# The last attention step of a Flamingo block in an order of its own

## The chip, the cores and the metric

The kernel runs on one core of a Trainium2 chip. The metric is the time of one execution on the device in microseconds (us); before the change it is 874.02 us, the median of three runs (873.65 to 874.04).

A core has a TensorE (matrix products and transposes; its weight loads are a row of their own, PEld), a VectorE (DVE), a ScalarE (ACT), a GpSimd (POOL) and a SyncE (SP), which starts transfers. Each works off its own list of instructions in order and waits on semaphores for the others.

## The reference

`x` is 2 batches of 2048 rows of 512, the context 2 batches of 77 rows. A gated cross-attention of 16 heads of width 32 is followed by a gated feed-forward layer:

```python
x = x + tanh(g_xattn[0]) * xattn(layernorm(x), ctx, ctx, Wq, Wk, Wv, Wo)
x = x + tanh(g_ffn[0]) * ffn(layernorm(x), w_gate, w_up, w_down)
# xattn: softmax of (q k^T * HD**-0.5) over the 77 context rows, causal mask, times v, times Wo^T
# ffn:   silu(x wg^T) * (x wu^T), times wd^T; integer weights, scaled by 1/127
```

## The kernel before

Products of float32 values are made from a high part (rounded to fp32r) and a low part (the rest): ACT writes the high part of a result in PSUM to SBUF, DVE subtracts it from PSUM for the low part, and TensorE makes three products (high by high, low by high, high by low).

The 4096 rows go in NB = 8 blocks of 512, and a block in TT = 4 tiles of 128 rows. A block's **step** has four kinds of work on each tile t:

- **scores**: `score_unit(n, t, u)` makes six products of 308 columns for heads 0 to 7 (unit 0, PSUM banks 0 and 1) or 8 to 15 (unit 1, banks 2 and 3). Each unit has one pair of banks, so a tile's unit waits until the tile before it is out: unit 0 for the shift on DVE (`s0_shifted`), unit 1 for the exponentials on ACT (`exp1_done`).
- **softmax**. Unit 0: DVE takes the maxima (`mx`, L1073), subtracts them into `e` in SBUF (L1076, `shift0`), ACT makes one exponential of 616 columns (`exp0`, L784), DVE sums and inverts (`denominator0`). Unit 1: DVE takes the maxima (L1084, `largest1`) and makes their scaled negative (`nmx`, L1090, `offset1`), ACT makes eight exponentials of 77 columns straight from PSUM, with the sums (`exp1`, L791), DVE inverts them (L1114, `denominator1`). POOL multiplies `e` by the inverse, unit by unit (L554, `weigh`).
- **transposes** of the weighed `e` in three pieces, `p(t, 0)` and `p(t, 1)` of four 128-column transposes and `p(t, 2)` of two, through two PSUM banks in turn. ACT copies each piece to `pT` (L764), DVE makes its low part (L1047); only that frees the bank for the piece after the next. `p(t, 0)` waits for the weighing of unit 0, `p(t, 1)` for that of unit 1.
- **output slices** `o(t)` (`project`): twelve products of 512 columns of `aT`, the weighed values of the block before, with `Wo`, added to `x_res` by DVE (L1120, `residual`).

At the head of a step stand the products of the block before's probabilities with V (36 products, `values`); between the transposes of the other steps stand also the query products of the next block. The last step (n = 7) has no query products. In their place it has `turn`: 16 transposes of normalised rows `x2` for the feed-forward layer into PSUM banks 0 to 3, which wait for the last tile's exponentials; POOL normalises `x2` in this step (L679). After the last step come the values and output slices of block 7, then the feed-forward layer, whose products (L1814, L1864) fill the time to the end.

The order on each engine is written out by hand, in `step` of each engine's program. On DVE the order within a tile is: `shift` (both units), `p(t-1, 0)`, `denominator0`, `p(t-1, 1)`, an output slice, `denominator1`, `p(t-1, 2)`, and then the next tile. The functions and lines are these:

Of the kernel before, what the change touches and what calls it, by code (L numbers as in the profile page):

```python
# [5 lines left out]
def flamingo_gated_block(  # L6
# [34 lines left out]
    P = 128  # L41
# [65 lines left out]
    with ctx:  # L107
# [396 lines left out]
        def _(pool):  # L504
# [166 lines left out]
            def normalise_first(i):  # L671

                c = slice(TT * i, TT * i + TT)
                nc.gpsimd.tensor_scalar(nmean2[:, c], mv2[:, c, 0], -1.0, 0.0, ALU.mult, ALU.add).then_inc(nmean_ready, 1)
                pool.wait_ge(nmean_ready, i + 1)
                pool.wait_ge(rstd2_ready, i + 1)
                for t in range(TT):
# [7 lines left out]
            normalise_first(0)  # L685
            probabilities(NB - 1, 1)
            normalise_first(1)
            probabilities(NB - 1, 2)
            probabilities(NB - 1, 3)
# [40 lines left out]
        def _(act):  # L730
# [136 lines left out]
            def step(n, query):  # L867
                def p(t, r):
                    p_high(n, t, r, 3 * t + r)

                def weighted(m):
                    m_high(m_base(n) + m, m, aT[:, 0, m, :])

                exp0(n, 0)
                weighted(0)
                exp1(n, 0, lambda: weighted(1))
                weighted(2)
                weighted(3)
                if query:
                    for k in range(KD):  # L880
                        x_high_t(n + 1, k)
                q_at = m_base(n) + 8

                def q(m):
                    if query:
                        m_high(q_at + m, m, qT[:, 0, m, :])

                for t in (1, 2):
                    p(t - 1, 0)
                    exp0(n, t)  # L890
                    p(t - 1, 1)
                    exp1(n, t)
                    p(t - 1, 2)
                p(2, 0)
                exp0(n, 3)
                p(2, 1)
                exp1(n, 3, lambda: q(0))
                p(2, 2)
                if not query:
                    act.wait_ge(var_out, 16 * MH)  # L900
                    xv_copy(0, B11, b11_at)
                q(1)
                q(2)
                p(3, 0)
                q(3)
                p(3, 1)
                if not query:
                    b12_copy(0)
                p(3, 2)
# [23 lines left out]
            with act.Fori(1, NB - 1) as n:  # L933
                step(n, True)
            step(NB - 1, False)
# [93 lines left out]
        def _(dve):  # L1029
# [242 lines left out]
            def step(n, query, ahead):  # L1272
                def p(t, r):
                    p_low(n, t, r, 3 * t + r)

                def st(t):
# [7 lines left out]
                    elif query and not ahead:  # L1284
                        stats2(t // TT, t % TT)

                def q(m):
                    if query:
                        q_low(h_base(n) + 5 + m, m)
# [13 lines left out]
                p(0, 0)  # L1303
                denominator0(n, 1)
                p(0, 1)
                residual(n, 0)
                denominator1(n, 1)
                p(0, 2)
                st(0)
                if query:  # L1310
                    residual(n, 1)
                slot_free(n, 2)
                shift(n, 2)
                p(1, 0)
                denominator0(n, 2)
                p(1, 1)
                residual(n, 2 if query else 1)
                denominator1(n, 2)
                p(1, 2)
                st(1)  # L1320
                if query:
                    residual(n, 3)
                slot_free(n, 3)
                shift(n, 3)
                p(2, 0)
                denominator0(n, 3)
                p(2, 1)
                st(2)
                q(0)
                if not query:  # L1330
                    residual(n, 2)
                denominator1(n, 3)
                p(2, 2)
                if not query:
                    residual(n, 3)
                st(3)
                if not query:
                    xv_low(0, B11, b11_at)
# [4 lines left out]
                p(3, 0)  # L1343
# [3 lines left out]
                p(3, 1)  # L1347
                p(3, 2)
                if not query:
                    form(0, T1)  # L1350
# [608 lines left out]
```

## Time and profile before

| | |
|---|---|
| runs, median (lowest to highest) | 874.02 us (873.65 to 874.04) |
| the profiled execution, whole | 874.07 us |
| its span in the profile | 872.3 us |
| busy share of the span: PE, PEld, DVE, ACT, POOL | 98%, 81%, 75%, 53%, 46% |
| granted TensorE clock, mean | 1.00 (2.4 GHz) in every slice |
| the last step's first score product, first values product after the step, first feed-forward product | 313.11, 350.57 and 372.39 us |

The profile counts from the span's start. A row of the timeline gives the start, the time from the start of its first to the end of its last instruction, engine, line, operation, the tiles, the count, and in brackets how long the engine was idle before it and what released it. TensorE's ends are modelled, and the next product starts before the one before it has ended, so for TensorE the distance between two starts is the better measure.

### The profile page before, as it was taken

To read this page: it belongs to the slowest core of one execution; us is meant where nothing else is said; L and a number is where in the kernel's file an instruction comes from. 1 tells how busy PE (TensorE), PEld (TensorE's weight loads), DVE (VectorE), ACT (ScalarE), POOL (GpSimd) and SP (SyncE) were. 2 spreads that over 40 slices of the span, in tenths; PEclk is the share of its full clock that TensorE was granted. 3 is DMA by queue.
4 is the path that set the end of the run, shared out by engine and by line. 5 is a ranking of instruction groups with operands and counts; after the bars stand their busy time and mean duration, and the time that the engine had idled before them with its cause. 6 is when DMAs were issued, how large, how long until landed. Compare 5 with 4: busy or idle time off the path is not lost.

```text
span 872.3 us, 12869 instructions
## 1 busy us (share of the span) xinstructions
PE 855.0 (98%) x4087; PEld 707.9 (81%) x4087; DVE 652.8 (75%) x1081; ACT 460.5 (53%) x1130; POOL 402.3 (46%) x344
## 2 busy tenths in 40 slices
PE   8999999999999999999999999999999999999997
PEld 7678888888888887788888888888888888888876
DVE  5988877778786877679688478788487877587882
ACT  5687575666666757446056264165362364460550
POOL 4665555556564664437144444155253255251350
PEclk9999999999999999999999999999999999999999
DMA  9233847272728131567333256043265143243302
GB/s 334 73 109 118 276 152 248 84 240 93 233 97 277 68 113 51 198 235 265 115 123 133 96 190 249 12 165 121 79 248 182 47 164 113 96 166 116 97 31 98
DMA packets 60406, 128.73 MB, mean 148 GB/s; under 512 B 7616, under 2 KB 20416, under 8 KB 60352
## 3 DMA queue, kind: packets, MB, share of 16 engines
q1 hardware_dynamic: 58960, 125.95, 41.7%
q10 hardware_dynamic: 1392, 2.10, 0.7%
q8 instruction: 29, 0.48, 0.2%
q14 instruction: 25, 0.20, 0.1%
HBM read 99.93 MB, written 27.79 MB: 146 GB/s over the span
## 4 chain that ended last, share of the span: by engine, by line
PE 87%; DVE 6%; ACT 3%; issue 1%; DMA 1%; POOL 1%; ACTq 0%; DVEq 0%
PE psum L1814 34%; PE psum L1548 29%; PE psum L1864 18%; PE psum L1573 4%; DMA gates<-g_ffn 1%; PE psum L1657 1%; ACT e L791 1%; POOL hT L696 1%; DVE bn L1034 1%; DVE e L1076 1%; DVE K L1128 1%; DVE mx L1073 1%; DVE qT L1058 0%; DVE pT L1047 0%; DVE aT L1058 0%
## 5 line engine op out<-in xcount | busy, mean ns | idle before, releaser
L1814 PE MATMUL psum<-xv,ring 128*128 128x512 f32 x1344 | 308.2, 390 | 0.9 <-ACT a L964 0.7
L1814 PEld LDWEIGHTS psum<-xv,ring 128*128 128x128 f32 x1344 | 251.5, 188 | 55.1 <-ACT a L964 1.1
L696 POOL TENSOR_TENSOR hT<-th,hT 128x512 fp32r<-128x512 f32 x48 | 86.3, 1798 | 201.2 <-ACT hT L984 201.2
L1864 PE MATMUL psum<-w_d,hT 128*128 128x512 f32 x768 | 177.7, 391 | 1.3 <-POOL hT L696 0.8
L1864 PEld LDWEIGHTS psum<-w_d,hT 128*128 128x128 f32 x768 | 143.7, 188 | 32.6 <-POOL hT L696 2.0
L554 POOL TENSOR_TENSOR e<-e,rden 128x616 f32<-128x616 f32 x64 | 77.9, 1217 | 110.4 <-DVE rden L1110 73.8
L791 ACT ACTIVATE e<-psum,nmx,q_scale 128x77 f32<-128x77 f32 x256 | 102.6, 427 | 2.3 <-DVE nmx L1090 2.2
L952 ACT ACTIVATE a<-psum 128x512 f32<-128x512 f32 x48 | 28.7, 599 | 131.7 <-PE psum L1814 131.4
L1428 DVE SCALAR_TENSOR_TENSOR acc<-psum,gate_ffn,acc 128x512 f32<-128x512 f32 x64 | 47.7, 750 | 65.1 <-PE psum L1864 65.1
L1548 PE MATMUL psum<-wo,aT 128*128 128x512 f32 x384 | 95.2, 399 | 0.5 <-DVE aT L1058 0.5
L1548 PE MATMUL psum<-xT,wq 128*128 128x512 f32 x360 | 89.0, 398 | 0.4 <-DVE qT L1058 0.4
L1548 PEld LDWEIGHTS psum<-wo,aT 128*128 128x128 f32 x384 | 70.0, 188 | 14.6 <-DVE aT L1058 0.8
L1548 PEld LDWEIGHTS psum<-xT,wq 128*128 128x128 f32 x360 | 65.6, 188 | 14.6 <-DVE qT L1058 1.9
L696 POOL TENSOR_TENSOR hT<-c,hT 128x512 fp32r<-128x512 f32 x48 | 62.1, 1293 | 22.4 <-ACT hT L984 22.4
L764 ACT ACTIVATE pT<-psum 128x512 fp32r<-128x512 f32 (+1 forms) x96 | 49.8, 531 | 36.2 <-PE psum L1573 36.2
L1548 PE MATMUL psum<-pT,V 128*128 128x512 f32 x288 | 68.1, 392 | 0.6 <-DVE aT L1058 0.6
L1548 PE MATMUL psum<-K,qT 128*128 128x308 f32 x384 | 63.7, 310 | 2.1 <-ACT e L791 2.1
L1548 PEld LDWEIGHTS psum<-pT,V 128*128 128x128 f32 x288 | 53.3, 188 | 12.5 <-DVE aT L1058 1.1
L1548 PEld LDWEIGHTS psum<-K,qT 128*128 128x128 f32 x384 | 56.8, 189 | 6.5 <-ACT e L791 3.0
L1392 DVE SCALAR_TENSOR_TENSOR th<-th,c 128x512 f32<-128x512 f32 x48 | 56.0, 1166 | 7.1 <-ACT th L977 4.3
L984 ACT ACTIVATE hT<-th 128x512 fp32r<-128x512 f32 x48 | 30.4, 633 | 53.9 <-DVE th L1405 53.9
L1047 DVE TENSOR_TENSOR pT<-psum,pT 128x512 fp32r<-128x512 f32 (+1 forms) x96 | 55.6, 588 | 2.5 <-ACT pT L764 1.0
(110 smaller groups left out, 1204.6 us busy)
## 6 DMA issues: line engine op xcount, KB each, us to landing
ring<-w_var SPq DMA_DIRECT2D x48, 896.0 KB, 4.6
w_var<-stage SPq DMA_DIRECT2D x12, 896.0 KB, 4.6
x_ln<-x SPq DMA_DIRECT2D x32, 256.0 KB, 4.6
x_res<-x SPq DMA_DIRECT2D x32, 256.0 KB, 5.0
x_mid<-x_res SPq DMA_DIRECT2D x32, 256.0 KB, 2.0
x<-x_mid SPq DMA_DIRECT2D x16, 512.0 KB, 5.6
acc<-x_mid SPq DMA_DIRECT2D x16, 512.0 KB, 6.4
out<-acc SPq DMA_DIRECT2D x32, 256.0 KB, 2.0
```

The source lines that it names most:

```text
L554: nc.gpsimd.tensor_tensor(e[:, t % 2, hs], e[:, t % 2, hs], rden[:, t % 2, hs].unsqueeze(2).to_broadcast([P, UH, SK]), ALU.mult).then_inc( ...
L696: nc.gpsimd.tensor_tensor(hT[:, 1, i % HH, j, :], h[:, :], hT[:, 0, i % HH, j, :].bitcast(f32), ALU.subtract).then_inc(h_lo, 1)
L764: nc.scalar.activation(dst, src, ACT.Copy).then_inc(t_hi, 1)
L791: last = nc.scalar.activation(e[:, t % 2, UH + h, :], s_bank[1][:, h // HG, (h % HG) * SK:(h % HG + 1) * SK], ACT.Exp, bias=nmx[:, t % 2, ...
L984: nc.scalar.activation(hT[:, 0, i % HH, j, :], h[:, :], ACT.Copy).then_inc(h_hi, 1)
L1047: nc.vector.tensor_tensor(dst, src, hi.bitcast(f32), ALU.subtract).then_inc(t_free, 1)
L1392: nc.vector.scalar_tensor_tensor(th2[:, :], th2[:, :], 1.0, c22[:, :], ALU.add, ALU.mult)\
L1428: nc.vector.scalar_tensor_tensor(acc[:, t, :], m_bank[t % 2][:, :], gate_ffn[:, 0:1], acc[:, t, :], ALU.mult, ALU.add).then_inc(m_free, 1)
L1548: last = nc.tensor.matmul(dst, stat, mov, start=(j == 0), stop=(j == len(terms) - 1))
L1573: last = nc.tensor.transpose(t_bank[at % 2][:, j * P:(j + 1) * P], rows[:, start:start + P], ident[:, :])
L1814: last = nc.tensor.matmul(psum[:, bank, :], stat, mov, start=start and j == 0, stop=j == len(terms) - 1, skip_group_check=not start)
L1864: last = nc.tensor.matmul(m_bank[t % 2][:, :], hT[:, a, m, t // TT, (t % TT) * P:(t % TT + 1) * P], w_d[:, HH * h + m, :], start=m == 0 an ...
```

## The change

Only the last step changes. It gets functions of its own on ACT, DVE and TensorE (`last_step`), and POOL's work there is put in another order; the loops of the other steps issue what they did. In the last step:

- TensorE: a tile's scores are no longer twelve products in a row. Unit 1 of tile t+1 stands behind `p(t, 0)`, unit 0 of tile t+2 behind `p(t, 2)`. An output slice goes in two halves of six products, one before `p(t, 1)` and one behind the scores of unit 0. `p(3, 0)` and the whole of `o(3)` stand ahead of `turn`.
- DVE: `p(t, 0)` stands between the shift of unit 0 and the maxima of unit 1; `p(t, 1)` and `p(t, 2)` stand together behind `denominator0`; `denominator1(t)` stands behind the shift of tile t+1, and the output slices one tile later.
- ACT: `p(t-1, 1)` is copied in the middle of the eight exponentials of tile t instead of ahead of them; `p(3, 0)` ahead of the copy of the turned rows.
- POOL: the negated means are made first; the second four normalisations of `x2` go in two pairs between weighings.

```diff
+                for t in (1, 2, 3):                       # ACT, last_step
+                    p(n, t - 1, 0)
+                    exp0(n, t)
+                    exp1(n, t, lambda: p(n, t - 1, 1))
+                    p(n, t - 1, 2)
...
+                for t in range(TT - 1):                   # DVE, last_step
+                    slot_free(n, t + 1)
+                    shift0(n, t + 1)
+                    if t:
+                        denominator1(n, t)
+                    p(n, t, 0)
+                    largest1(n, t + 1)
+                    offset1(n, t + 1)
+                    denominator0(n, t + 1)
+                    if t:
+                        residual(n, t - 1)
+                    p(n, t, 1)
+                    p(n, t, 2)
+                residual(n, 2)
+                p(n, 3, 0)
+                denominator1(n, 3)
+                residual(n, 3)
+                xv_low(0, B11, b11_at)
+                p(n, 3, 1)
+                p(n, 3, 2)
+                form(0, T1)
...
+                weigh_values(n, b, b, False)              # TensorE, last_step
+                score_unit(n, 1, 0, b, False)
+                for t in range(TT - 1):
+                    p(n, t, 0)
+                    score_unit(n, t + 1, 1, b, False)
+                    if t == 0:
+                        pe.wait_ge(m_free, base + 4)
+                    o(t, early)
+                    p(n, t, 1)
+                    p(n, t, 2)
+                    if t + 2 < TT:
+                        score_unit(n, t + 2, 0, b, False)
+                    o(t, late)
+                p(n, 3, 0)
+                o(3, range(G))
+                turn(0, B11)
+                turn(0, B12)
+                p(n, 3, 1)
+                p(n, 3, 2)
...
+            mean_first(0)                                 # POOL
+            mean_first(1)
             probabilities(NB - 1, 0)
+            normalise_first(0, range(TT))
+            weigh(NB - 1, 1, 0)
+            normalise_first(1, range(0, 2))
+            weigh(NB - 1, 1, 1)
+            weigh(NB - 1, 2, 0)
+            normalise_first(1, range(2, 4))
+            weigh(NB - 1, 2, 1)
+            weigh(NB - 1, 3, 0)
+            weigh(NB - 1, 3, 1)
```

The order on DVE before, from the last low part of tile 0 (`pT` of 2x128) to the offset of tile 2's unit 1 and what follows it. `mx` are maxima, `e` the shifted scores, `nmx` the offset, `rden` an inverse sum:

```order
L1114 RECIPROCAL rden<-den 128x8 [waits exp1_done]
L1047 TENSOR_TENSOR pT<-psum,pT 128x2x128 [waits t_hi]
L1073 TENSOR_REDUCE mx<-psum 128x8 [waits s0_full,t_full]
L1076 TENSOR_TENSOR e<-psum,mx 128x308 [waits mx0_done]
L1076 TENSOR_TENSOR e<-psum,mx 128x308
L1084 TENSOR_REDUCE mx<-psum 128x8 [waits s1_full]
L1090 SCALAR_TENSOR_TENSOR nmx<-mx,q_scale,minus 128x8 [waits mx1_done,scale_ready]
L1047 TENSOR_TENSOR pT<-psum,pT 128x4x128 [waits t_hi]
```

The same place on DVE now:

```order
L1067 TENSOR_TENSOR pT<-psum,pT 128x2x128 [waits t_hi]
L1093 TENSOR_REDUCE mx<-psum 128x8 [waits s0_full,t_full]
L1096 TENSOR_TENSOR e<-psum,mx 128x308 [waits mx0_done]
L1096 TENSOR_TENSOR e<-psum,mx 128x308
L1134 RECIPROCAL rden<-den 128x8 [waits exp1_done]
L1067 TENSOR_TENSOR pT<-psum,pT 128x4x128 [waits t_hi]
L1104 TENSOR_REDUCE mx<-psum 128x8 [waits s1_full]
L1110 SCALAR_TENSOR_TENSOR nmx<-mx,q_scale,minus 128x8 [waits mx1_done,scale_ready]
```

The inverse of tile 1's unit 1 moved from ahead of the shift of tile 2 to behind it, and it and the low part of `p(1, 0)` now stand ahead of the maxima and the offset of tile 2's unit 1. The low part of `p(0, 2)` still stands ahead of the shift.

The order on ACT before, from the shifted exponential of tile 2 to the last copy of tile 1 (`e,den` are the eight exponentials):

```order
L784 ACTIVATE e<-e,q_scale 128x616 [waits s0_shifted,scale_ready]
L764 ACTIVATE pT<-psum 128x4x128 [waits t_full]
L791 ACTIVATE e,den<-psum,nmx,q_scale 128x77 [waits nmx_ready]
L791 ACTIVATE e,den<-psum,nmx,q_scale 128x77 x7
L764 ACTIVATE pT<-psum 128x2x128 [waits t_full]
```

The same place on ACT now:

```order
L793 ACTIVATE e<-e,q_scale 128x616 [waits s0_shifted,scale_ready]
L800 ACTIVATE e,den<-psum,nmx,q_scale 128x77 [waits nmx_ready]
L800 ACTIVATE e,den<-psum,nmx,q_scale 128x77 x3
L773 ACTIVATE pT<-psum 128x4x128 [waits t_full]
L800 ACTIVATE e,den<-psum,nmx,q_scale 128x77 x4
L773 ACTIVATE pT<-psum 128x2x128 [waits t_full]
```

The copy of `p(1, 1)` moved from ahead of the eight exponentials to their middle; the copy of `p(1, 2)` stays behind the eighth.

The order on TensorE before, from tile 1's transposes to the last scores (`K,qT` are scores, `ident,e` transposes, `wo,aT` an output slice):

```order
L1573 MATMUL psum<-ident,e 128x128 [waits t_free,p0_ready]
L1573 MATMUL psum<-ident,e 128x128 x3
L1573 MATMUL psum<-ident,e 128x128 [waits t_free,p1_ready]
L1573 MATMUL psum<-ident,e 128x128 x3
L1548 MATMUL psum<-wo,aT 128x512 [waits m_free]
L1548 MATMUL psum<-wo,aT 128x512 x11
L1573 MATMUL psum<-ident,e 128x128 [waits t_free]
L1573 MATMUL psum<-ident,e 128x128
L1548 MATMUL psum<-K,qT 128x308 [waits s0_shifted]
L1548 MATMUL psum<-K,qT 128x308 x5
L1548 MATMUL psum<-K,qT 128x308 [waits exp1_done]
L1548 MATMUL psum<-K,qT 128x308 x5
```

The same place on TensorE now:

```order
L1613 MATMUL psum<-ident,e 128x128 [waits t_free,p0_ready]
L1613 MATMUL psum<-ident,e 128x128 x3
L1588 MATMUL psum<-K,qT 128x308 [waits exp1_done]
L1588 MATMUL psum<-K,qT 128x308 x5
L1657 MATMUL psum<-wo,aT 128x512 [waits m_free]
L1657 MATMUL psum<-wo,aT 128x512 x5
L1613 MATMUL psum<-ident,e 128x128 [waits t_free,p1_ready]
L1613 MATMUL psum<-ident,e 128x128 x3
L1613 MATMUL psum<-ident,e 128x128 [waits t_free]
L1613 MATMUL psum<-ident,e 128x128
L1588 MATMUL psum<-K,qT 128x308 [waits s0_shifted]
L1588 MATMUL psum<-K,qT 128x308 x5
```

The scores of unit 1, which wait for the exponentials of the tile before, moved from behind the output slice to behind `p(t, 0)`, and have half a slice behind them.

## Rows read from the trace of the kernel before

**Rows 1.** The page, busy time, share of the span and instructions of each engine

```profile
PE 855.0 (98%) x4087; PEld 707.9 (81%) x4087; DVE 652.8 (75%) x1081; ACT 460.5 (53%) x1130; POOL 402.3 (46%) x344
```

**Rows 2.** Timeline of TensorE over the last step: start, length, [idle before]

```profile
331.62 1.11 PE L1548 MATMUL psum<-K,qT 128*128 128x308 f32 x6 [1.19 <-ACT e L791]
...
338.51 1.13 PE L1548 MATMUL psum<-K,qT 128*128 128x308 f32 x6 [0.86 <-ACT e L791]
...
343.45 3.02 PE L1548 MATMUL psum<-wo,aT 128*128 128x512 f32 x12
...
350.38 0.44 PE L1573 MATMUL psum<-ident,e 128*128 128x128 f32 x2 [1.29 <-DVE pT L1047]
350.57 4.37 PE L1548 MATMUL psum<-pT,V 128*128 128x512 f32 x18
```

**Rows 3.** Chain that ended last, last step, in order of time: start, length

```profile
331.87 0.04 DVE pT L1047
...
332.21 0.80 DVE mx L1073
...
333.03 0.87 DVE e L1076 x2
...
335.29 3.18 ACT e L791 x16
```

**Rows 4.** Timeline of ACT: first exponentials of three tiles, copies around the second

```profile
328.28 0.41 ACT L791 ACTIVATE e<-psum,nmx,q_scale 128x77 f32<-128x77 f32 x1
...
334.71 0.58 ACT L764 ACTIVATE pT<-psum 128x512 fp32r<-128x512 f32 x1
335.18 0.41 ACT L791 ACTIVATE e<-psum,nmx,q_scale 128x77 f32<-128x77 f32 x1
...
338.33 0.40 ACT L764 ACTIVATE pT<-psum 128x256 fp32r<-128x256 f32 x1
...
342.08 0.41 ACT L791 ACTIVATE e<-psum,nmx,q_scale 128x77 f32<-128x77 f32 x1
```

**Rows 5.** Timeline of DVE: offsets of tiles 1 and 2, then tile 3

```profile
327.80 0.23 DVE L1090 SCALAR_TENSOR_TENSOR nmx<-mx,q_scale,minus 128x8 f32<-128x8 f32 x1
...
334.71 0.23 DVE L1090 SCALAR_TENSOR_TENSOR nmx<-mx,q_scale,minus 128x8 f32<-128x8 f32 x1
...
338.76 0.42 DVE L1047 TENSOR_TENSOR pT<-psum,pT 128x256 fp32r<-128x256 f32 x1
339.11 0.79 DVE L1073 TENSOR_REDUCE mx<-psum 128x8 f32<-128x616 f32 x1
...
340.71 0.79 DVE L1084 TENSOR_REDUCE mx<-psum 128x8 f32<-128x616 f32 x1
341.61 0.23 DVE L1090 SCALAR_TENSOR_TENSOR nmx<-mx,q_scale,minus 128x8 f32<-128x8 f32 x1
341.75 0.68 DVE L1047 TENSOR_TENSOR pT<-psum,pT 128x512 fp32r<-128x512 f32 x1
342.35 0.78 DVE L1108 TENSOR_REDUCE den<-e 128x8 f32<-128x616 f32 x1
343.17 0.20 DVE L1110 RECIPROCAL rden<-den 128x8 f32<-128x8 f32 x1
343.29 0.64 DVE L1047 TENSOR_TENSOR pT<-psum,pT 128x512 fp32r<-128x512 f32 x1
```

**Rows 6.** Timeline of POOL: four normalisations and a weighing in the last step

```profile
333.36 3.02 POOL L679 TENSOR_SCALAR x<-x,nmean,rstd 128x512 f32<-128x512 f32 x4
...
338.77 1.22 POOL L554 TENSOR_TENSOR e<-e,rden 128x616 f32<-128x616 f32 x1 [1.00 <-DVE rden L1114]
```

**Rows 7.** Timeline of SP's queue: reload of the rows for block 7's output slices

```profile
349.12 2.13 SPq L393 DMA_DIRECT2D x_res<-x  x4
```

**Rows 8.** Transfers issued from 345 to 362 us: KB each, us to landing

```profile
x_res<-x SPq DMA_DIRECT2D x4, 256.0 KB, 8.4
```

**Rows 9.** Timeline of DVE: first output slice of block 7

```profile
364.42 0.75 DVE L1120 SCALAR_TENSOR_TENSOR x_res<-psum,gate_t,x_res 128x512 f32<-128x512 f32 x1 [1.27 <-PE psum L1548]
```

More of the change, by code:

```diff
@@ L865, in first_block, with p @@
                 p(3, 2)
[L867 to L872, printed above, removed]
-                exp0(n, 0)
[L875 to L881, printed above, removed]
+            def p(n, t, r):
+                p_high(n, t, r, 3 * t + r)
@@ L1270, in xv_low, with p, step @@
                     .then_inc(xb_lo, 1)
[L1272 to L1274 removed]
+            def p(n, t, r):
+                p_low(n, t, r, 3 * t + r)
+            def step(n, ahead):
                 def st(t):
@@ L1610, in values, with project @@
                         ).then_inc(m_full, 1)
-            def project(i, t):
-                m_wait(i)
-                product(m_bank[t % 2][:, :],
-                        [(aT[:, a, m, t * P:(t + 1) * P], wo[:, c, m, :]) for m in range(G) for a, c in CROSS]
-                        ).then_inc(m_full, 1)
+            def project(i, t, groups=range(G)):
+                if groups[0] == 0:
+                    m_wait(i)
+                for m in groups:
+                    for a, c in CROSS:
+                        last = nc.tensor.matmul(m_bank[t % 2][:, :], aT[:, a, m, t * P:(t + 1) * P], wo[:, c, m, :],
+                                                start=m == 0 and a + c == 0, stop=m == G - 1 and c == 1)
+                if groups[-1] == G - 1:
+                    last.then_inc(m_full, 1)
             pe.wait_ge(const_step, 2)
@@ L1736, in first_block, with p, weigh_values, step @@
                 p(3, 2)
-            def step(n, b, b_before, masked, more):
+            def p(n, t, r):
+                transpose_p(n, t, r, 3 * t + r)
+            def weigh_values(n, b, b_before, masked):
+                scores(n, 0, b, masked, (m_base(n) - 2, m_base(n)))
+                for m in range(G):
+                    values(m_base(n) + m, m, b_before, t_base(n) - 2 + min(m, 2))
+            def step(n, b, b_before, masked):
                 base = m_base(n)
-                def p(t, r):
-                    transpose_p(n, t, r, 3 * t + r)
                 def o(t):
@@ L1747, in q @@
                 def q(m):
-                    if more:
-                        query(base + 8 + m, m)
-                scores(n, 0, b, masked, (base - 2, base))
-                for m in range(G):
-                    values(base + m, m, b_before, t_base(n) - 2 + min(m, 2))
+                    query(base + 8 + m, m)
+                weigh_values(n, b, b_before, masked)
                 scores(n, 1, b, False)
-                p(0, 0)
-                p(0, 1)
+                p(n, 0, 0)
+                p(n, 0, 1)
                 pe.wait_ge(m_free, base + 4)
```

171 lines of the change are left out of this document (88 added, 83 removed).

## The prediction

> **What bounds the kernel now.** I read the page's busy shares first: TensorE 98%, no other engine over 75% [rows 1]. A change gains only where TensorE stands, and it can lose wherever it makes TensorE stand longer. Then the timeline of TensorE over the last step, for its idle times: 1.19 us and 0.86 us before the scores of tiles 2 and 3, unit 1, both ended by ACT's exponentials of the tile before, and 1.29 us before the two last transposes, ended by a low part on DVE; the values products of block 7 begin at 350.57 [rows 2]. So 3.34 us are there to be had, 0.38% of the time. Then the chain of waits, to see what sets these stands: the low part of the two-piece product, the maxima and the shift of unit 0, and the eight exponentials follow one another, across DVE and ACT, round and round [rows 3]. ACT's timeline gives the loop's length: the first exponentials of tiles 1, 2 and 3 start at 328.28, 335.18 and 342.08, 6.90 us apart each time [rows 4]. This loop is the bound of the step, not TensorE.
>
> **The loop after the change, step by step.** ACT copies `p(t-1, 2)` only behind the eighth exponential of tile t, as before; DVE works in order, and its low part of that piece still stands ahead of the next shift. So "the shift sooner" holds for the scores that feed it, not for the shift. From one tile's first exponential to the next one's:
> - the eight exponentials, 338.33 - 335.18 = 3.15 [rows 4];
> - the copy of `p(t-1, 1)`, new in their middle: 335.18 - 334.71 = 0.47 [rows 4];
> - the copy of the two-piece part until DVE takes it: 338.76 - 338.33 = 0.43 [rows 4, 5];
> - its low part, 339.11 - 338.76 = 0.35 [rows 5];
> - maxima and shift of unit 0, 340.71 - 339.11 = 1.60 [rows 5];
> - the inverse of unit 1, now behind the shift: 343.29 - 343.17 = 0.12 (a reciprocal of the same size) [rows 5];
> - the low part of `p(t, 0)`, now ahead of the offset: 342.35 - 341.75 = 0.60 [rows 5];
> - maxima of unit 1 until the offset, 341.61 - 340.71 = 0.90 [rows 5];
> - the offset and the hand-over to ACT, 0.23 + 0.03 = 0.26 [rows 5].
>
> The sum is 7.88 us against 6.90. Before, the exponential of unit 0 and a copy on ACT ran beside the maxima and the offset; now they still do, and have ended a microsecond before the offset, so they hide nothing and cost nothing. What grew the loop are three things put on it: a copy between exponentials, a low part and an inverse before the offset.
>
> **Where the loop starts and where it meets TensorE.** In tile 1 the offset started at 327.80 and now stands behind the low part of `p(0, 0)`: 327.80 + 0.60 + 0.23 + 0.03 = 328.66 for the first exponential, 0.38 later than before. Tile 3's then starts at 328.66 + 2 x 7.88 = 344.42 (before 342.08). Behind its fourth exponential ACT copies `p(2, 1)`: 3.15 / 2 + 0.58 + 0.03 = 2.19 later [rows 4]; DVE's low part of it takes 0.68 [rows 5] and 0.05 of hand-over, and only that frees the bank for `p(3, 0)`, at 344.42 + 2.92 = 347.34. This is the new wait on TensorE. Queued behind it there are `o(3)`, the sixteen turns and six transposes, and then the values. The same instructions stood between 343.45 and 350.57 before, 7.12 us with 1.29 idle, so 5.83 of work [rows 2]. The values now start at 347.34 + 5.83 = 353.17, which is 2.60 later.
>
> TensorE is free by then. Tile 2's first exponential is at 336.54; the scores of tile 3 start 3.33 + 0.47 later (338.51 - 335.18, and the copy [rows 2, 4]), at 340.34, and with half a slice last until about 342.8. `p(2, 1)` waits for its weighing: behind the eighth exponential come 0.43 + 0.35 + 1.60 + 0.20 + 0.08 on ACT and DVE and 1.22 on POOL [rows 6], so until 344.0. Two transposing pieces and half a slice more end near 346.5, before 347.34. So there are new waits of about 1.4 us before `p(1, 1)` and `p(2, 1)`, but they lie beside the loop and not on top of it. The two old waits on exponentials shrink to some 0.3 us, the old one of 1.29 us at the end goes, since `p(3, 0)` now stands ahead of the turns.
>
> **The other parts.** The split slices issue the same twelve products, in the same banks. The pairs of normalisations on POOL (3.02 / 4 = 0.76 each [rows 6]) end before the weighing they stand ahead of can start. The reordered means are two tiny instructions. I take all of it as nothing, covered by POOL's idle second; uncovered, a pair would cost its 1.5 us. After the values, everything hangs on TensorE and moves with it. The reload of `x_res` waits for the last output slice of the step, which ended at 343.45 + 3.02 = 346.47 and now ends near 350.8, 4.3 later. The last piece was issued at 351.25 and landed some 8.4 later [rows 7, 8], at 359.7; now near 364.0. Its user, at 364.42 before [rows 9], moves by 2.6 to 367.0. It stays hidden, with 3.0 us left of 4.8.
>
> **A rule of the skill against this.** DVE's offset takes 0.23 us with POOL in the midst of its normalisations (334.71 against 333.36 to 336.38) and 0.23 with POOL idle (341.61) [rows 5, 6]. The Trainium skill, "SBUF — State Buffer", section "Who interferes with whom", says that a DVE instruction with two SBUF inputs contends with a GpSimd instruction that reads SBUF, and that whichever starts second blocks fully. The offset has two inputs in SBUF; the trace does not agree for this size. By that rule the moved weighings could stop it.
>
> **The sum.** The profiled execution took 874.07 us, 1.8 more than its span. 874.07 + 2.60 = 876.67; by the median of the runs, 874.02, it is 876.62. I say 876.6.
>
> **Rivals.**
> - *The loop gets short, not slower (873.1).* If the shift of tile t+1 ran beside the exponentials of tile t, only the exponentials until the next scores (338.51 - 335.18 = 3.33 [rows 2, 4]) with the copy (0.47), the scores (1.11 [rows 2]), and maxima and offset (1.16) with 0.05 of hand-over would be in it: 6.12 us. The values would start at 328.66 + 2 x 6.12 + 2.92 + 5.83 = 349.65, 0.9 sooner. For it: unit 0's scores are made earlier now. Against it: DVE's low part of `p(t-1, 2)`, which waits for the end of the exponentials, stands ahead of the shift. It decides from a loop under 6.58 us, where the values start at 350.57.
> - *Only the end changes (874.7).* If the added pieces found cover I don't see, the loop stayed at 6.90 and only the later start remained, the values would start at 328.66 + 13.80 + 8.75 = 351.21, 0.64 later: 874.7. Against it: DVE shows no idle time between 338.76 and 343.29 [rows 5].
> - *The waits add to the loop (877.6).* Every stand of TensorE costs a slow first product behind it, and there are about seven instead of four; and if `p(2, 1)`'s weighing came 1.9 us later than I put it, TensorE would reach `p(3, 0)` late by 1.0. For it: POOL has a pair of normalisations ahead.
> - *The port rule (880.3).* Three offsets, each stopped by a whole weighing of 1.22 [rows 6], make 3.7 more. The 0.23 beside a busy POOL speaks against it.
>
> **How the numbers follow.** The forecast has 0.80 (its own range 875.8 to 877.2: each of nine durations off by 5% moves it by some 0.3, the hand-overs and the slow first products by as much), the short loop 0.05, only the end 0.08, the adding waits 0.06, the port rule 0.01. What this measurement can tell from no change is about 0.2%, 1.75 us: slower is over 875.8, which is nearly all of the forecast and the two last, 0.84; within it lie the "only the end" case, most of the short loop, and a low tail, 0.13; faster needs more than 1.75 us of the 3.34 and nearly all waits gone, which even the short loop does not give: 0.03. The range that leaves 2 in 10 out at most is 875.0 to 877.5.
>
> **What would show it.** In the new profile: first exponentials of tiles 1, 2 and 3 near 328.7, 336.5 and 344.4; DVE's shift of each tile directly behind the two-piece low part; TensorE idle about 1.4 us before `p(1, 1)` and `p(2, 1)`, about 1 us before `p(3, 0)`, and no wait before the last two transposes; the values products from 353.2. It is wrong if the exponentials come 6.9 us apart or less, if the shift runs during the exponentials, or if the values start before 351.5.

## The result, and the profile after

| | before | after |
|---|---|---|
| runs of this comparison, median (lowest to highest) | 873.58 us (873.11 to 874.04, 12 runs) | 876.11 us (875.51 to 877.09, 12 runs) |
| ratio of the times, 95% interval | | 1.0030 (1.0021 to 1.0039) |
| the profiled execution, whole, and its span | 874.07 and 872.3 us | 875.89 and 874.1 us |
| first values product after the last step | 350.57 us | 353.12 us |
| first feed-forward product | 372.39 us | 374.91 us |

The change makes the kernel 2.5 us slower, three parts in a thousand. The forecast was 876.6 us, with the values at 353.17. The profiled pair differs by 1.8 us only, though the feed-forward layer starts 2.52 us later in it; from there to the end of the span it took 499.9 us before and 499.2 after, and these 0.7 us are less than what separates the lowest run of one kernel from the highest. The place in the trace where the values start is therefore a sharper measure of an edit in this step than the whole time, and I use both. It has a drift of its own: the step's first score product starts between 312.79 and 313.25 us in the profiles here (313.11 before, 313.22 after), so differences under half a microsecond between two runs are read only counted from that product. So counted, the values are 2.44 us later after the change (39.90 against 37.46).

The page of the kernel after shows nothing of it, as [rows 1] did not:

```profile
PE 855.2 (98%) x4087; PEld 707.0 (81%) x4087; DVE 652.7 (75%) x1081; ACT 461.0 (53%) x1130; POOL 403.1 (46%) x344
```

The loss is in the timeline of TensorE over the last step (start, length, instructions, idle time before in brackets), which answers to [rows 2]:

```profile
331.84 0.63 PE L1613 MATMUL psum<-ident,e 128*128 128x128 f32 x4 [1.28 <-DVE pT L1067]
332.61 1.11 PE L1588 MATMUL psum<-K,qT 128*128 128x308 f32 x6
...
336.36 0.87 PE L1613 MATMUL psum<-ident,e 128*128 128x128 f32 x6 [1.26 <-POOL e L554]
...
339.69 0.63 PE L1613 MATMUL psum<-ident,e 128*128 128x128 f32 x4 [0.22 <-DVE pT L1067]
...
344.21 0.87 PE L1613 MATMUL psum<-ident,e 128*128 128x128 f32 x6 [1.25 <-POOL e L554]
...
347.54 0.63 PE L1613 MATMUL psum<-ident,e 128*128 128x128 f32 x4 [1.07 <-DVE pT L1067]
347.93 3.03 PE L1657 MATMUL psum<-wo,aT 128*128 128x512 f32 x12
350.80 1.91 PE L1701 MATMUL psum<-ident,x 128*128 128x128 f32 x16
...
353.12 4.34 PE L1588 MATMUL psum<-pT,V 128*128 128x512 f32 x18
```

The 1.29 us at the end are gone, as announced, and the timeline names no wait on exponentials any more. Five waits took their place: before `p(1, 0)`, `p(1, 1)`, `p(2, 0)`, `p(2, 1)` and `p(3, 0)`, together 5.08 us where there were 3.34. Two more hide behind the modelled ends: four transposes and the scores behind them start 0.77 us apart at 331.84 (and at 339.69), and 0.35 us apart where nothing is waited for (`p(0, 0)`, 324.85, and its scores, 325.20). So the scores of tiles 2 and 3, unit 1, still wait 0.42 us each; the timeline of the weight loads names the wait:

```profile
332.61 0.87 PEld L1588 LDWEIGHTS psum<-K,qT 128*128 128x128 f32 x6 [0.38 <-ACT e L800]
```

With these two the waits that I can name have grown by 2.58 us. The loop behind them is in ACT's timeline of the kernel after (answers to [rows 4]), at the first exponentials of tiles 1, 2 and 3:

```profile
328.78 0.42 ACT L800 ACTIVATE e<-psum,nmx,q_scale 128x77 f32<-128x77 f32 x1 [0.77 <-DVE nmx L1110]
...
336.63 0.42 ACT L800 ACTIVATE e<-psum,nmx,q_scale 128x77 f32<-128x77 f32 x1 [0.83 <-DVE nmx L1110]
...
338.22 0.60 ACT L773 ACTIVATE pT<-psum 128x512 fp32r<-128x512 f32 x1
...
344.48 0.42 ACT L800 ACTIVATE e<-psum,nmx,q_scale 128x77 f32<-128x77 f32 x1 [0.83 <-DVE nmx L1110]
```

They are 7.85 us apart both times, where they were 6.90. DVE's timeline for tile 2 (answers to [rows 5]) shows the order that makes it so; the chain of waits of the kernel after, round tile 1's exponentials, goes through the same instructions:

```profile
334.03 0.86 DVE L1096 TENSOR_TENSOR e<-psum,mx 128x308 f32<-128x308 f32 x2
334.81 0.19 DVE L1134 RECIPROCAL rden<-den 128x8 f32<-128x8 f32 x1
334.92 0.64 DVE L1067 TENSOR_TENSOR pT<-psum,pT 128x512 fp32r<-128x512 f32 x1
335.48 0.79 DVE L1104 TENSOR_REDUCE mx<-psum 128x8 f32<-128x616 f32 x1
336.37 0.23 DVE L1110 SCALAR_TENSOR_TENSOR nmx<-mx,q_scale,minus 128x8 f32<-128x8 f32 x1
```

```profile
330.97 1.59 ACT e L800 x8
332.56 0.28 ACT pT L773
332.87 0.04 DVE pT L1067
332.90 0.31 issue
333.21 0.80 DVE mx L1093
334.03 0.86 DVE e L1096 x2
334.89 0.11 DVE rden L1134
335.00 0.56 DVE pT L1067
335.56 0.72 DVE mx L1104
```

DVE goes without a gap from the shift to the offset, and the inverse and the low part of `p(1, 0)` stand between them. In the chain the second half of the exponentials is followed by the copy and the low part of the two-piece product, and only then by the maxima of the next tile.

### The profile page after: what moved, and what is told of

Same layout as the page of the kernel before. It is cut to its first block, busy times and chain, and to the rows that moved or that the text cites. A ratio compares the mean times of both kernels' runs of the same rounds, so it can differ in the third digit from the quotient of the medians.

```text
span 874.1 us, 12870 instructions
## 1 busy us (share of the span) xinstructions
PE 855.2 (98%) x4087; PEld 707.0 (81%) x4087; DVE 652.7 (75%) x1081; ACT 461.0 (53%) x1130; POOL 403.1 (46%) x344
## 4 chain that ended last, share of the span: by engine, by line
PE 86%; DVE 7%; ACT 3%; issue 1%; DMA 1%; POOL 1%; ACTq 0%; DVEq 0%
PE psum L1877 34%; PE psum L1588 20%; PE psum L1927 18%; PE psum L1657 9%; PE psum L1613 4%; DMA xs<-x_t 1%; ACT e L800 1%; PE psum L1701 1%; DVE e L1096 1%; POOL hT L705 1%; DVE bn L1054 1%; DVE mx L1093 1%; DVE pT L1067 1%; DVE K L1148 1%; DVE mx L1104 1%
```

## The experiments

A plain estimate in the expectations adds or takes away single terms of the prediction's sum. The "layout" places every instruction of the last step by its order on its engine and its waits, with the durations of the trace of before; it is arithmetic on those rows, and only its results are given, in the expectations. Each time stands beside runs of the kernel before on the same chip (873.5 to 873.9 us).

**The shift ahead of the two-piece low part.** From the kernel after, DVE's low part of `p(t-1, 2)` goes behind the next shift and the inverse:

```diff
                     shift0(n, t + 1)
                     if t:
                         denominator1(n, t)
+                        p(n, t - 1, 2)
                     p(n, t, 0)
...
                     p(n, t, 1)
-                    p(n, t, 2)
+                p(n, 2, 2)                 # behind the loop
```

> The changed kernel with one move on DVE: the low part of the two-piece product p(t-1, 2) stands behind the shift of tile t+1 (and behind the inverse) instead of ahead of it. My theory (the loop over DVE and ACT sets the step; that low part holds the shift back until the exponentials are over): the shift now runs during the exponentials, the 0.43 + 0.35 + 1.60 us of it leave the loop and ACT's and DVE's other work takes their place; first exponentials about 6.6 us apart instead of 7.85, no wait left before p(1, 1) and p(2, 1), values products from about 350.6 instead of 353.1, time about 873.6. Rival (TensorE's own new order costs the time, the loop only follows it): no gain, 876.1. Rival (the three pieces put on the loop cost all of it, and the place of the shift nothing): 876.1 as well.

Measured: 873.52 us (872.97 to 875.39), ratio 1.0002 (0.9993 to 1.0011). First exponentials at 328.79, 335.37 and 341.95, 6.58 us apart instead of 7.85; values at 350.52 instead of 353.12. The timeline of TensorE:

```profile
331.84 0.63 PE L1614 MATMUL psum<-ident,e 128*128 128x128 f32 x4 [1.29 <-DVE pT L1067]
...
338.42 0.63 PE L1614 MATMUL psum<-ident,e 128*128 128x128 f32 x4 [0.41 <-DVE pT L1067]
...
345.00 0.63 PE L1614 MATMUL psum<-ident,e 128*128 128x128 f32 x4 [1.23 <-DVE pT L1067]
```

The two waits on POOL's weighings are gone with it; ACT, POOL and TensorE are those of the kernel after. A round is 1.27 us shorter, and the values come 2.60 us sooner, near two rounds' worth (2.54): the loop sets the time of the step. But this does not undo a part of the change. In the kernel before, the low part of `p(t-1, 2)` stands ahead of the shift too, and its loop has 6.90 us. One move of DVE's makes up for the whole loss; what caused the loss, the pieces new on the loop, is tested further down, one by one.

**And the maxima and the offset ahead of both low parts:**

```diff
                     shift0(n, t + 1)
                     if t:
                         denominator1(n, t)
-                    p(n, t, 0)
                     largest1(n, t + 1)
                     offset1(n, t + 1)
+                    if t:
+                        p(n, t - 1, 2)
+                    p(n, t, 0)
...
                     p(n, t, 1)
-                    p(n, t, 2)
+                p(n, 2, 2)                 # behind the loop
```

> As the one before, and the maxima and offset of unit 1 also stand ahead of both low parts, so that nothing but the inverse lies between the shift and them. My theory: 0.60 + 0.35 leave the loop too; first exponentials about 6.1 apart, values from about 349.2, time about 872.2, below the kernel before. Rival (TensorE's own order): 876.1. Rival (only the shift's place matters, the pieces ahead of the offset lie in ACT's idle time): as the run before, 873.6.

Measured: 872.15 us (871.52 to 873.05), ratio 0.9984 (0.9975 to 0.9993); exponentials 6.13 and 6.15 us apart, values at 348.86. So the new order on TensorE is worth something once DVE lets the loop go.

**Only the low part of `p(t, 0)` behind the offset**, the rest as after:

```diff
-                    p(n, t, 0)
                     largest1(n, t + 1)
                     offset1(n, t + 1)
+                    p(n, t, 0)
```

> The changed kernel with one move on DVE: the low part of p(t, 0) stands behind the offset of unit 1, as before the change; the shift stays where the change has it. My theory by the plain terms: 0.60 less twice in the loop and 0.60 less at its start, so 1.8 less: values from about 351.3, time 874.3. Rival (TensorE's own order): 876.1. Rival (the term is hidden by the exponential of unit 0 and the copies on ACT, which now end 0.8 before the offset): up to the whole 1.8 is lost, at least 0.8 of each 0.6 is not, so this rival can only hold if ACT has more work there than I see: 876.1.

Measured: 874.49 us (874.05 to 875.36), ratio 1.0014 (1.0004 to 1.0023), values at 351.77. The term of 0.60 is real: tile 1's first exponential comes 0.60 us sooner, counted from the step's first score product. But the rounds are 7.58 us where 7.85 less 0.60 is 7.25; what makes the 0.33 is told below, with POOL's timeline.

**ACT's copy of `p(t-1, 1)` ahead of the exponentials again**, the rest as after:

```diff
-                    exp1(n, t, lambda: p(n, t - 1, 1))
+                    p(n, t - 1, 1)
+                    exp1(n, t)
```

> The changed kernel with one move on ACT: the copy of p(t-1, 1) stands ahead of the eight exponentials again, not in their middle. By the term of my prediction alone (0.47 on the loop) twice 0.47 would go: 875.2. Laid out in full, the copy then waits for its transposes, which now wait for the late weighing of unit 1 behind the late inverse, so it comes at the offset's heels and holds the exponentials back by as much as it frees: first exponentials 8.3 apart, but p(2, 1) copied earlier, values from about 352.8, time 875.8. Rival (TensorE's own order): 876.1. So the exponentials' distance in the trace tells the two terms apart: 7.4 by the term alone, 8.3 by the layout.

Measured: 875.65 us (875.23 to 877.39), ratio 1.0027 (1.0016 to 1.0039), values at 352.57; exponentials 8.28 us apart. Taking 0.47 out of the middle made the loop longer, since the copy now comes behind the wait for POOL's weighing (TensorE idle 1.27 <-POOL), and the exponentials behind the copy. The loop is a maximum over paths, and what one term of the longest path is worth can't be had by taking it away alone.

**Single parts put into the kernel before.** POOL's new order alone; TensorE's new order alone; on DVE only the low part of `p(t, 0)` between the shift and the maxima of unit 1; on ACT only the copy in the middle.

```diff
+            mean_first(0)                  # POOL alone
+            mean_first(1)
+            normalise_first(0, range(TT))
+            weigh(NB - 1, 1, 0)
+            normalise_first(1, range(0, 2))
+            ...
```

> The kernel before with POOL's new order alone (means first, the second four normalisations in two pairs between weighings). My prediction took these moves as nothing. By durations laid out: the pair ahead of the weighing of tile 1's unit 1 ends 1.2 + 1.5 after that of unit 0 starts, 0.5 us later than the old weighing could start, and again in tile 2: p(1, 1) and p(2, 1) wait 0.7 instead of 0.15, of which the scores of the next tile give back the first since they wait for ACT anyway: values 0.6 later, 874.2. If POOL's order costs nothing: 873.6.

```diff
+                last_step(NB - 1, B - 1)   # TensorE alone, as in the change
```

> The kernel before with TensorE's new order alone; DVE, ACT and POOL as before. Rival theory (TensorE's own order is what costs): the whole loss, 876.1. My theory too has a loss here, from the clash of orders: DVE takes the output slice 0 ahead of the low part p(0, 2), but TensorE makes it later, so the two last transposes of tiles 1 and 2 wait 1.4 and 1.6: values from about 353.2, 876.2. The two agree in the time and not in the place: by mine the stands are before p(1, 2), p(2, 2) and p(3, 2) and the exponentials are 7.0 to 7.3 apart.

```diff
+                    shift0(n, t + 1)       # DVE alone, last step
+                    p(t, 0)
+                    largest1(n, t + 1)
+                    offset1(n, t + 1)
```

> The kernel before with one of the change's three pieces alone: in the last step the low part of p(t-1, 0) stands ahead of the maxima of unit 1 instead of behind its offset. By the plain term, 0.60 on every round: first exponentials 7.50 apart, values from 350.57 + 0.6 x 3 = 352.4, time 875.4. By the durations laid out, the offset before had 0.25 of slack behind the copy on ACT, so the loop grows by 0.38 to 7.28, the start by 0.38, and the scores' waits take the rest: first exponentials 7.3 apart, values from about 351.5, time 874.5. If the loop over DVE and ACT isn't the bound: 873.5.

```diff
+                        exp1(n, t, lambda: p(t - 1, 1))   # ACT alone, last step
```

> The kernel before with another of the change's three pieces alone: on ACT, in the last step, the copy of p(t-1, 1) stands in the middle of the eight exponentials of tile t instead of ahead of them. By the plain term: 0.47 on every round, first exponentials 7.37 apart, values 1.4 later, 875.0. By the durations laid out, the exponentials start up to 0.25 earlier since the copy no longer stands ahead of them, and the offset on DVE binds in its place: rounds of 7.15, values 0.64 later, 874.2. If the loop isn't the bound: 873.6.

Measured, with the distances of the first exponentials (6.90 and 6.90 before) and the start of the values (350.57 before):

| alone in the kernel before | median (range) us | ratio (95%) | distances | values | from the step's first score, against 37.46 |
|---|---|---|---|---|---|
| POOL's order | 873.90 (873.69 to 874.52) | 1.0006 (0.9997 to 1.0015) | 6.90, 6.89 | 350.70 | 37.91 (+0.45) |
| TensorE's order | 875.99 (875.52 to 876.09) | 1.0028 (1.0017 to 1.0039) | 6.93, 7.32 | 352.73 | 39.80 (+2.34) |
| low part ahead | 874.53 (874.15 to 949.26, one run far out) | 1.0008 (0.9998 to 1.0017) | 7.44, 7.32 | 351.45 | 38.42 (+0.96) |
| copy in the middle | 874.21 (873.71 to 875.71) | 1.0009 (1.0000 to 1.0018) | 7.19, 7.19 | 350.89 | 38.03 (+0.57) |

POOL's order costs nothing that the times can tell from no change, but the trace has a cost: in the kernel before it gives the transposes of `p(1, 1)` and `p(2, 1)` waits of 0.45 us, and the wait of tile 3's scores falls from 0.86 to 0.38, so one of the two stays, 0.45 us on the values. In the kernel after the same order costs nothing, since POOL stands idle for 2.59 us ahead of both of these weighings (its timeline, at 335.09 and 342.94). The two single moves cost 0.42 (where POOL does not meet the offset) and 0.29 us a loop, and not their 0.60 and 0.47: before, ACT became free at 335.18, and DVE's offset had ended at 334.94 [rows 4, 5], so up to 0.24 us could be covered; 0.18 was, both times (0.60 - 0.42 and 0.47 - 0.29). In the whole change the three pieces, 0.47 + 0.12 + 0.60 = 1.19 us, made a round 0.95 longer, so there 0.24 was covered. The inverse (0.12) was not moved alone.

TensorE's order alone costs as much as the whole change. Its waits:

```profile
328.51 0.44 PE L1573 MATMUL psum<-ident,e 128*128 128x128 f32 x2 [0.72 <-DVE pT L1047]
...
335.82 0.44 PE L1573 MATMUL psum<-ident,e 128*128 128x128 f32 x2 [1.25 <-DVE pT L1047]
...
342.98 0.44 PE L1573 MATMUL psum<-ident,e 128*128 128x128 f32 x2 [1.39 <-DVE pT L1047]
...
352.54 0.44 PE L1573 MATMUL psum<-ident,e 128*128 128x128 f32 x2 [1.72 <-DVE pT L1047]
```

They stand at other places than in the kernel after: before the two-piece transposes, whose bank DVE's old order frees late. That raises a rival, that TensorE's order and not the loop over DVE and ACT is the cause. The next experiment is its test.

**The kernel after with TensorE's old order** (`step` issues `p(t, 0)`, `p(t, 1)`, a whole output slice, `p(t, 2)` and then both units' scores, as before):

> The changed kernel with TensorE's old order; DVE, ACT and POOL as changed. Rival theory (TensorE's own order is what costs): back to about 873.6. My theory (the loop over DVE and ACT costs, and TensorE's new order softens it by putting work behind the waits): the loop stays at 7.9, and every stand of TensorE gets longer since twelve products no longer stand between: values 3.2 later than in the changed kernel, 879.3.

Measured: 883.07 us (881.94 to 884.15), ratio 1.0115 (1.0100 to 1.0131), values at 359.14. The rival, at 873.6, is out: with the other engines as changed TensorE's old order is 7 us worse than the new one. A good part of that is a clash at the step's end: DVE now takes the inverse of tile 3's unit 1 behind the low part of `p(3, 0)`, which TensorE's old order makes only behind `o(3)` and the turns, at 355.09, so the weighing and `p(3, 1)` come late (a wait of 2.82 us, named for POOL). The time is also 3.8 us more than I expected, and the values come 2.8 later than the layout had them (3.2 behind those of the kernel after). TensorE's timeline, and its stretches of 4 us (start and end, length, busy time and count of PE, PEld, DVE, ACT and POOL, granted clock, DMA share, GB/s):

```profile
332.43 1.60 PE L1588 MATMUL psum<-K,qT 128*128 128x308 f32 x6 [2.07 <-ACT e L800]
333.82 1.05 PE L1613 MATMUL psum<-ident,e 128*128 128x128 f32 x4
336.18 1.12 PE L1613 MATMUL psum<-ident,e 128*128 128x128 f32 x4 [1.30 <-POOL e L554]
336.94 4.27 PE L1588 MATMUL psum<-wo,aT 128*128 128x512 f32 x12
...
345.96 4.59 PE L1588 MATMUL psum<-wo,aT 128*128 128x512 f32 x12
```

```profile
328.00:332.00 4.00, 2.36 (x14) 1.85 (x12) 2.06 (x5) 3.41 (x16) 2.41 (x3) 1.00 0.00 0
332.00:336.00 4.00, 2.45 (x10) 2.02 (x10) 2.56 (x6) 1.73 (x5) 1.41 (x2) 0.60 0.00 0
336.00:340.00 4.00, 3.82 (x12) 3.21 (x13) 3.18 (x7) 2.90 (x13) 1.82 (x3) 0.54 0.08 30
340.00:344.00 4.00, 3.57 (x24) 3.06 (x22) 2.23 (x6) 1.87 (x8) 1.04 (x2) 1.00 0.13 44
344.00:348.00 4.00, 2.45 (x10) 2.06 (x11) 3.34 (x8) 2.99 (x11) 2.24 (x2) 0.81 0.00 0
```

Behind an idle of 2.07 us the granted clock fell from 2.4 to 1.2 GHz for most of 8 us, and after one of 1.98 us once more. Two output slices of twelve products took 4.27 and 4.59 us, where one takes 3.02 [rows 2]: 1.25 and 1.57 more, 2.82 together, about what the values are late against the layout. The loop grew too: its rounds are 8.72 and 8.68 us, where I expected 7.9.

**The same with the waits filled.** To see whether the clock alone makes the difference, 14, 12 and 14 products of 128 columns of the identity, written to a free bank and read by nobody, stand before the scores of tile 2's unit 1, before `p(1, 1)` and before `p(2, 1)`; then, as shorter lots, 8, 6 and 7.

```diff
+                    fill(1, 8)             # first 14, then 8: matmul(m_bank, ident, ident), 128 columns
                     score_unit(n, 2, 1, b, False)
```

> The run before with TensorE's old order took 883.1 where the laid-out durations gave 879.3; its trace shows a granted clock of 0.60 and 0.54 from 332 to 340 us, behind an idle time of 2.07. This kernel is the same, with 40 small products (128 columns, into a PSUM bank that nobody reads) put into three of TensorE's waits: 14 ahead of the scores of tile 2, unit 1, 12 ahead of p(1, 1), 14 ahead of p(2, 1). Each lot is shorter than its wait at full clock. If the lower clock made the excess, the clock stays at 1.00 and the time comes down to about 879.5, values from about 356.6, with more work than before. If the layout was wrong there (the order costs more than I see), the time stays at 883.1 or rises.

> The filled kernel again, since its lots were too long: a filler took 0.235 us there, not 0.11 (14 of them 3.3 us against a wait of 2.07). Now 8, 6 and 7 fillers (1.9, 1.4 and 1.65 us), each lot shorter than its wait. If the lower clock made the excess of the kernel with TensorE's old order over its layout: clock 1.00 throughout, values from about 356.6 instead of 359.1, time about 879.6 instead of 883.1. If the layout was wrong there: values still from about 359, 883.1.

Measured: 882.06 us (881.01 to 883.06), ratio 1.0095 (1.0080 to 1.0111), with the long lots. The clock stayed at 1.00, but a product took 0.22 us from start to start (two records each), so a lot of fourteen took 3.0 to 3.1 us and was longer than the wait: this run decides little. With the short lots 880.25 us (878.95 to 880.71), ratio 1.0073 (1.0059 to 1.0086), and the values at 356.17, where I expected 356.6. With the clock at 1.00 through the step, the rounds are 7.85 and 7.91 us again, and the values come 2.97 us sooner than without the fillers: the orders as they clash here make 5.6 us of lateness against the kernel before, and the clock made the rest. It fell this time behind the wait that I had left unfilled, and the values' first eighteen products took 5.99 us instead of 4.37 [rows 2]:

```profile
355.54 0.87 PE L1613 MATMUL psum<-ident,e 128*128 128x128 f32 x6 [2.82 <-POOL e L554]
356.17 5.99 PE L1588 MATMUL psum<-pT,V 128*128 128x512 f32 x18
```

```profile
352.00:356.00 4.00, 1.18 (x11) 0.94 (x10) 2.55 (x4) 1.51 (x2) 1.22 (x1) 1.00 0.08 30
356.00:360.00 4.00, 4.00 (x15) 3.19 (x14) 2.24 (x3) 2.01 (x4) 0.00 (x0) 0.61 0.99 348
```

**All four engines' orders, laid out together.** On DVE the shift goes ahead of whatever only frees banks, and ahead of the offset stand only low parts for which there is time while the scores of unit 1 are made; on TensorE an output slice or half of one stands wherever the layout had a wait; POOL's normalisations go in ones, twos and threes between weighings; ACT's order (not shown) has the copies behind the exponentials, but for tile 3.

```diff
+                shift0(n, 2)               # DVE, the core of it
+                p(n, 0, 1)
+                p(n, 0, 2)
+                denominator1(n, 1)
+                residual(n, 0)
+                largest1(n, 2)
+                offset1(n, 2)
+                denominator0(n, 2)
+                p(n, 1, 0)
+                residual(n, 1)
+                slot_free(n, 3)
+                shift0(n, 3)
...
+                o(0, early)                # TensorE, the core of it
+                score_unit(n, 2, 0, b, False)
+                p(n, 0, 2)
+                o(0, late)
+                o(1, early)
+                score_unit(n, 2, 1, b, False)
+                p(n, 1, 0)
+                o(1, late)
+                score_unit(n, 3, 0, b, False)
```

> All four engines in an order found by laying out the durations of the trace so that TensorE never waits in the step: shift of tile t+1 during the exponentials of tile t, maxima and offset directly behind the inverse, low parts and output slices behind them, the normalisations in single pieces between weighings, the copies of p(t, 1) behind the exponentials. My theory (all waits are set by the orders on DVE and ACT, TensorE's work is the floor): values from about 346.4, 4.2 sooner than before and 6.7 sooner than after the change, 869.4. Rival (a loop over the engines that no order can shorten): not below 873.6.

Measured: 870.02 us (869.78 to 871.40), ratio 0.9964 (0.9951 to 0.9978): 3.5 us below the kernel before and the fastest here. The values start at 346.80, 3.77 us sooner than before (3.58 counted from the step's first score), and from the second tile's scores on TensorE's timeline names no wait in the step any more (by the distances of the starts three of 0.15 to 0.32 us are left). Its end:

```profile
343.78 0.82 PE L1639 MATMUL psum<-ident,e 128*128 128x128 f32 x6
344.45 1.94 PE L1727 MATMUL psum<-ident,x 128*128 128x128 f32 x16
346.22 0.82 PE L1639 MATMUL psum<-ident,e 128*128 128x128 f32 x6
346.80 4.34 PE L1614 MATMUL psum<-pT,V 128*128 128x512 f32 x18
```

## Why the prediction was right, point by point

- *The loop, 7.88 us.* Measured 7.85, twice. That it goes through DVE's low part of the two-piece product and the shift behind it is shown by moving that low part: 6.58 us, and the values come sooner by two rounds' gain. The kernel before has that low part at the same place, so the loss itself is the added pieces: 1.19 us by my sum, 0.95 in the trace, since before the change 0.24 us of them had cover. Two of the three cost 0.42 and 0.29 us alone.
- *The start, 328.66.* Measured 328.78, and 0.11 of the 0.12 is the drift from ahead of the step.
- *`p(3, 0)` at 347.34, behind it 5.83 of work, values at 353.17.* Measured 347.54, 5.58 and 353.12; the two errors nearly cancel, which is luck. The 0.25 of the second is in how I read the rows: I took the idle 1.29 us out of a stretch, but they count from a modelled end. The eight transposes ahead of that wait last 1.03 us to this end, and the same eight, with no wait behind them, 0.79 from start to start (325.55 to 326.34), so the work was 5.59.
- *New waits.* About 1.4 us before `p(1, 1)` and `p(2, 1)`: 1.26 and 1.25 (my own figures, 342.8 and 344.0, give 1.2). About 1 us before `p(3, 0)`: 1.07. At the end none: none. Some 0.3 us on the scores of unit 1: 0.42. One miss: 1.28 and 0.22 us before `p(1, 0)` and `p(2, 0)`, where DVE's low part of the bank's last piece is late. They lie beside the loop and moved nothing.
- *POOL at nothing.* It holds for the kernel after, where POOL is idle for 2.59 us ahead of both moved weighings, far more than the "idle second" I counted on. In the kernel before, the same order costs 0.45 us in the trace, too little for the times to show (1.0006, 0.9997 to 1.0015).
- *The reload of `x_res` hidden.* SP's queue issued it from 353.60 to 355.84 us, a transfer landed some 8.5 later, so by about 364.3, and its user on DVE started at 366.94 [rows 9 answer to it] behind a wait for TensorE; I had put it at 367.0.
- *The rivals.* The short loop needed the shift beside the exponentials; with that order it was measured, at 6.58 us with the low part of `p(t, 0)` still ahead of the offset and 6.14 without it (I had 6.12). "Only the end" fell with the 7.85, and "the waits add" with the values at 353.12: `p(2, 1)`'s weighing was over at 344.16, 0.2 and not 1.9 us behind my 344.0.
- *The port rule: the right verdict for a wrong reason.* I read the 0.23 us of the offset beside busy POOL [rows 5, 6] as evidence that the two don't meet. It was not. The four normalisations run from 333.36 for 3.02 us, so the second ended near 334.87 (an estimate, a quarter of the 3.02 each), before the offset's 0.23 us were over; a stop until then would not have shown. The same trace has the stop. Of its 32 offsets (minimum, median and maximum in ns) one took 1149 ns, and ended with the weighing beside it:

```profile
L1090 DVE SCALAR_TENSOR_TENSOR nmx<-mx,q_scale,minus x32: 225/227/1149, 28.9 to 341.6; 128x8 f32<-128x8 f32 x32
```

```profile
42.58 1.15 DVE L1090 SCALAR_TENSOR_TENSOR nmx<-mx,q_scale,minus 128x8 f32<-128x8 f32 x1 [0.17 <-PE psum L1573]
```

```profile
42.49 1.22 POOL L554 TENSOR_TENSOR e<-e,rden 128x616 f32<-128x616 f32 x1 [2.04 <-DVE rden L1114]
```

Offset and weighing end at 43.73 and 43.71. In the kernel after, the offset of tile 2 starts at 336.37, and the weighing beside it, from 335.09 for 1.22 us, has ended at 336.31; for tile 3 it is 344.22 and 344.16. The rule cost nothing because both offsets began 0.06 us after the weighing had ended, and nothing in my working knew that. That was luck, and the chance of 0.01 for this rival was too small. With the low part behind the offset, the offset comes sooner and is caught, DVE's timeline and POOL's:

```profile
334.98 0.55 DVE L1110 SCALAR_TENSOR_TENSOR nmx<-mx,q_scale,minus 128x8 f32<-128x8 f32 x1
```

```profile
334.30 1.22 POOL L554 TENSOR_TENSOR e<-e,rden 128x616 f32<-128x616 f32 x1 [1.99 <-DVE rden L1134]
```

It ends at 335.53, the weighing at 335.52. The 0.32 us above its usual 0.23 is what was missing in that loop (tile 3's offset took 0.55 too): 7.25 + 0.32 = 7.57, and 7.58 was measured. In the laid-out kernel two offsets took 0.65 and 0.52 us and end 0.02 and 0.01 us behind a weighing and a normalisation; those 0.71 us exceed the 0.4 by which its values come later than laid out. What a kernel without this stop would take was not tried. The Trainium skill, "SBUF — State Buffer", section "Who interferes with whom", had it right: a DVE instruction with two SBUF inputs contends with a GpSimd instruction that reads SBUF, and the order of issue decides which of them waits. In these rows it was the offset, issued second.

## What to carry to other kernels

Where engines hand one another work in a loop, write the loop down with every instruction that stands in order on it, and put first on each engine what the next round waits for; what only frees a buffer goes behind it, even if its input has long been there. Feeding such a loop's first input earlier gains nothing while one in-order neighbour still stands ahead of its use, and a new order on one engine has to be judged with the others' (TensorE's new order: alone +2.4 us; with the other engines as changed +2.5, where TensorE's old order had +9.5; with two of DVE's moves more -1.4). A short duration beside a busy neighbour proves no absence of contention: look at the longest of all such instructions in the trace, and at what ended with it.

## What the runs showed of the hardware that I had not expected

- DVE's offset of 128x8 elements, 0.23 us, was held up to 1.15 us by an instruction of POOL under way. All six of the 32 in the trace of before that took over 0.25 us ended 0.02 to 0.04 us behind the end of an instruction of POOL.
- The granted clock stayed at 2.4 GHz through idle times of TensorE of 1.3 us, and fell to 1.2 GHz for several microseconds behind ones of 2.07 and 1.98 us, in a stretch in which TensorE also stood at other times. Behind the one wait of 2.8 us before the last transposes it fell in one run (0.61 in the 4 us after it) and stayed at 1.00 in two others with the same wait; what decides it stays open. Twelve products of 512 columns then took 4.27 to 4.59 us instead of 3.02. So each of the two waits of about 2 us cost another 1.25 or 1.57 us behind it.
- A float32 product of 128 columns of the identity is two records and takes 0.22 us from start to start, with the clock at 1.00.
